# Twelve places for tiles of V, the statistics of the first four steps placed one by one in SP's queue, and a new order of the run-in

## The reference

```python
x = x + attention(layernorm(x)); x = x + fp4_ffn(layernorm(x))
x = x + mixer_and_mlp(x);        x = x + time_mix_ffn(layernorm(x))

q, k, v = (h @ w for w in (w_q, w_k, w_v))          # 2048 x 1024 each, 16 heads of 64
allowed = same segment of 64 | (|i - j| a multiple of 4, 0 < |i - j| <= 256)
out = softmax(q k^T / 8 where allowed) v @ w_o
```

## Time and profile before

| | us |
|---|---|
| median of 3 runs | 515.27 |
| lowest, highest | 514.61, 518.27 |
| the profiled execution | 517.63 |
| its span, first to last instruction | 515.6 |
| TensorE busy, share of the span | 453.7, 88% |
| VectorE busy | 419.0, 81% |
| ScalarE busy | 349.9, 68% |
| GpSimd busy | 312.2, 61% |
| mean granted clock of TensorE | 0.977 of full speed |

### The profile page before, as it was taken

The page is one execution under the profiler, slowest core; times in us unless marked ns, Lnnn a source line. Parts: engine busy times, 40 slices in busy tenths (PEclk is TensorE's granted clock), DMA queues, the critical chain, the costliest instruction groups (busy, mean ns, idle before and its releaser), DMA issues.

```text
span 515.6 us, 17268 instructions
## 1 busy us (share of the span) xinstructions
PE 453.7 (88%) x6418; PEld 352.5 (68%) x6418; DVE 419.0 (81%) x1335; ACT 349.9 (68%) x1021; POOL 312.2 (61%) x497
## 2 busy tenths in 40 slices
PE   0899799999999999999999999989668789768996
PEld 0677577877878778778778788778335456346775
DVE  4865579897899999999999878868899977959135
ACT  3377468867777677677677687754534578786865
POOL 4123447777567577577576865555543789986420
PEclk9999899999999999999999999989879989989999
DMA  6267862346353353453464544540000000000002
GB/s 204 97 188 225 231 193 46 67 91 127 68 108 70 67 107 67 86 101 77 96 134 102 109 106 95 103 87 1 1 0 1 0 1 1 1 0 3 2 0 81
DMA packets 136099, 40.53 MB, mean 79 GB/s; under 512 B 104976, under 2 KB 131024, under 8 KB 136016
## 3 DMA queue, kind: packets, MB, share of 16 engines
q1 hardware_dynamic: 135440, 38.38, 32.2%
q10 hardware_dynamic: 576, 1.05, 0.5%
HBM read 29.44 MB, written 9.96 MB: 76 GB/s over the span
## 4 chain that ended last, share of the span: by engine, by line
PE 42%; DVE 28%; POOL 7%; issue 6%; ACT 6%; DMA 6%; SPq 4%; DVEq 0%; ACTq 0%; POOLq 0%
PE psum L449 6%; PE psum L407 5%; DVE pband L696 4%; PE psum L1153 4%; PE psum L469 3%; DVE pt L757 3%; PE psum L483 3%; PE psum L388 3%; PE psum L495 3%; PE psum L480 2%; DMA w_rows_dram<-st 2%; ACT pband L553 2%; DMA st<-w_rows_dram 2%; DVE area L1555 2%; PE psum L390 2%
## 5 line engine op out<-in xcount | busy, mean ns | idle before, releaser
L929 POOL TENSOR_SCALAR pband<-pband,fac 128x192 f32<-128x192 f32 x256 | 104.6, 429 | 98.7 <-DVE fac L748 98.6
L553 ACT ACTIVATE pband<-pband,st 128x192 f32<-128x192 f32 x256 | 113.2, 448 | 0.3 <-DVE st L696 0.3
L696 DVE CUSTOM_DVE_ANT_0 pband<-psum,band_mask 128x192 f32<-128x192 f32 x256 | 76.0, 353 | 2.6 <-PE psum L407 2.6
L407 PE MATMUL psum<-keys,q_class 64*64 64x192 f32 (+2 forms) x1536 | 66.3, 275 | 0.0
L449 PEld LDWEIGHTS psum<-ident,pband 128*128 128x128 f32 x384 | 45.2, 141 | 23.5 <-issue 18.0
L407 PEld LDWEIGHTS psum<-keys,q_class 64*64 64x64 f32 x1536 | 57.5, 133 | 2.3 <-issue 2.3
L449 PE MATMUL psum<-ident,pband 128*128 128x128 f32 x384 | 53.1, 274 | 3.9 <-DVE pt L757 3.9
L911 POOL COPY keys<-k_rows 128x512 f32<-128x512 f32 x32 | 36.6, 1143 | 24.2 <-issue 14.5
L553 ACT ACTIVATION_READ_ACCUMULATOR pband<-pband,st 128x1 f32 x256 | 49.3, 193 | 0.0
L757 DVE COPY pt<-psum 128x512 f32<-128x512 f32 x64 | 43.8, 684 | 2.0 <-PE psum L449 1.8
L919 POOL COPY q_class<-q_rows 128x512 f32<-128x512 f32 x32 | 36.2, 1131 | 10.3 <-ACT q_rows L593 10.3
(11 more groups left out here) (206 smaller groups left out, 1159.0 us busy)
## 6 DMA issues: line engine op xcount, KB each, us to landing
v_rows_dram<-arena SPq DMA_DIRECT2D x32, 256.0 KB, 3.3
v_both<-v_rows_dram SPq DMA_DIRECT2D x32, 256.0 KB, 3.7
v_seg<-v_rows_dram SPq DMA_DIRECT2D x64, 128.0 KB, 3.6
v_side<-v_rows_dram SPq DMA_DIRECT2D x96, 64.0 KB, 2.6
w_rows_dram<-st SPq DMA_DIRECT2D x64, 8.0 KB, 2.9
st<-w_rows_dram SPq DMA_DIRECT2D x64, 8.0 KB, 2.5
arena<-_attn_hidden_states_dram SPq DMA_DIRECT2D x4, 256.0 KB, 4.4
out_dram<-x SPq DMA_DIRECT2D x4, 256.0 KB, 2.5
```

What stands on the lines that cost most here:

```text
L407: return pe.matmul(bank[2 * r + head][rows, at:at + y.shape[1]], x, y, start=True, stop=True, skip_group_check=True)
L553: act.activation(x, x, ACT.Exp, bias=mine[:, head:head + 1], scale=-1.0, accum_out=mine[:, 2 + head:3 + head]).then_inc(s_exp, 1)
L696: dve.tensor_tensor_reduce(pband[:, G % P_SLOTS, c, head, :], bank[2 * r + head][:, at:at + BAND], band_mask[:, (0, 1, 1, 2)[w], SEG * (1 ...
L929: pool.tensor_scalar(x, x, fac[:, F % 2, 1, c, head:head + 1], 1.0, ALU.mult, ALU.mult).then_inc(s_scaled, 1)
```

## The change

`V_SLOTS` goes from 8 to 12. The four new places are the last 2048 columns of `arena`, behind w_q and w_k; `v_slot(i)` gives the place of a tile. Exchanges 2 and 3 leave SP's loop, which now begins at step 4; `send_statistics` and `fetch_statistics` of the steps 0 to 3 each have a place of their own among the stores and loads. The run-in's queues on all five engines get a new order. No operation is added or left out; each engine issues the same instructions, and `take_values(i)` waits for the store of tile i - 12 in place of i - 8.

```diff
--- before.py
+++ after.py
@@ -65,7 +65,7 @@
 PLAIN = 5 + 1 + 4 + 4 + 3
 W_ROWS = 3 * FT + PLAIN * P
 HALF_HD = HD // 2
-V_SLOTS = 8
+V_SLOTS = 12
 PT_SLOTS = 3
 P_SLOTS = 4
 ROW_SLOTS = 3
@@ -162,7 +162,6 @@
     x_in = pband[:, 2:4, :, :, :].rearrange("p s c h x -> p (s c h x)")[:, 0:NT * D].rearrange("p (n d) -> p n d", d=D)
     xc = pseg[:, 2:4, :, :, :].rearrange("p s a h x -> p s a (h x)")
     wv = pt[:, 0:2, :]
-    v_sb = arena[:, 0:V_SLOTS * 512].rearrange("p (k f) -> p k f", k=V_SLOTS)
     w_qk = arena[:, 4096:4096 + 2 * HD].rearrange("p (k f) -> p k f", k=2)
     wv_hi, wv_lo = w_hi[:, :, HALF_HD:HD], w_lo[:, :, HALF_HD:HD]
     raw = arena[:, 4096:4096 + 3 * FT].rearrange("p (m f) -> p m f", m=3)
@@ -208,6 +207,12 @@
 
         return i % NT, i // NT
 
+    def v_slot(i):
+
+        k = i % V_SLOTS
+        at = HALF_HD * k if k < 8 else 4096 + 2 * HD + HALF_HD * (k - 8)
+        return arena[:, at:at + HALF_HD]
+
     def there(n):
         return 0 <= n < NS_ALL
 
@@ -254,7 +259,7 @@
                 n, half = v_tile(i)
                 sp.wait_ge(s_vev[i % 2], i // 2 + 1)
                 sp.dma_start(v_rows[P * n:P * (n + 1), HALF_HD * half:HALF_HD * (half + 1)],
-                             v_sb[:, i % V_SLOTS, :]).then_inc(s_vst[i % V_SLOTS], 16)
+                             v_slot(i)).then_inc(s_vst[i % V_SLOTS], 16)
 
             def stored(half, w):
                 for i in range(NT * half + TW * w, NT * half + TW * (w + 1)):
@@ -309,21 +314,19 @@
             with nc.allow_non_contiguous_dma(reason="a column of 128 numbers"):
                 for k, v in enumerate(columns):
                     sp.dma_start(constants["cols"][:, k:k + 1], v.rearrange("(p o) -> p o", o=1)).then_inc(s_cols, 16)
-            store_v(0); store_v(1); store_v(2); store_v(3); store_v(4); store_v(5); load_own(0, 0); store_v(6)
-            store_v(7); store_v(8); load_own(0, 1); load_sides(0, 1); store_v(9); store_v(10); store_v(11)
-            store_v(12); store_v(13); load_own(0, 2); load_sides(0, 2); send_statistics(0); store_v(14); store_v(15)
-            store_v(16); store_v(17); store_v(18); store_v(19); fetch_statistics(0); store_v(20); store_v(21)
-            send_statistics(1); store_v(22); load_own(0, 3); load_sides(0, 3); load_wo(); fetch_statistics(1)
-            store_v(23); store_v(24); store_v(25); store_v(26); store_v(27); store_v(28); store_v(29); store_v(30)
-            store_v(31)
+            store_v(0); store_v(1); store_v(2); store_v(3); store_v(4); store_v(5); store_v(6); load_own(0, 0)
+            store_v(7); store_v(8); store_v(9); load_own(0, 1); store_v(10); load_sides(0, 1); send_statistics(0)
+            store_v(11); store_v(12); store_v(13); store_v(14); fetch_statistics(0); store_v(15); store_v(16)
+            store_v(17); load_own(0, 2); send_statistics(1); load_sides(0, 2); load_own(0, 3); load_sides(0, 3)
+            load_wo(); fetch_statistics(1); store_v(18); send_statistics(2); store_v(19); store_v(20); store_v(21)
+            store_v(22); store_v(23); store_v(24); store_v(25); store_v(26); store_v(27); fetch_statistics(2)
+            store_v(28); store_v(29); store_v(30); store_v(31); send_statistics(3); fetch_statistics(3)
             at = 0
-            for F in range(FIRST_STEP - 4, NS_ALL):
+            for F in range(NW, NS_ALL):
                 send_statistics(F)
-                if F >= NW:
-                    load_own(F // NW, F % NW)
+                load_own(F // NW, F % NW)
                 fetch_statistics(F)
-                if F >= NW:
-                    load_sides(F // NW, F % NW)
+                load_sides(F // NW, F % NW)
                 if F == RAW_STEP:
                     sp.wait_ge(s_zero, 1)
                 if F in (RAW_STEP, RAW_STEP + 1):
@@ -496,14 +499,14 @@
 
             pe.wait_ge(s_con, 2)
             pe.wait_ge(s_const, CONST)
-            turn_rows(0); values(0); values(1); turn_rows(1); values(2); project(0, 1); values(3); project(1, 1)
-            values(4); values(5); turn_rows(2); project(0, 0); values(6); values(7); turn_rows(3); values(8)
-            scores(0, 0); values(9); project(2, 1); values(10); project(1, 0); values(11); values(12); scores(0, 1)
-            values(13); project(3, 1); values(14); values(15); scores(1, 0); project(2, 0); values(16); values(17)
-            project(4, 1); values(18); values(19); scores(1, 1); scores(2, 0); values(20); values(21); project(3, 0)
-            values(22); values(23); scores(2, 1); values(24); values(25); project(5, 1); values(26); values(27)
-            project(4, 0); values(28); values(29); scores(3, 0); values(30); values(31); project(5, 0); turn(0, 0)
-            scores(3, 1); turn(0, 1); turn(0, 2)
+            turn_rows(0); values(0); values(1); turn_rows(1); values(2); project(0, 1); values(3); values(4)
+            project(1, 1); turn_rows(2); values(5); values(6); project(0, 0); values(7); values(8); project(2, 1)
+            scores(0, 0); project(1, 0); turn_rows(3); values(9); values(10); scores(0, 1); values(11); scores(1, 0)
+            project(3, 1); values(12); values(13); scores(1, 1); values(14); project(2, 0); values(15); values(16)
+            values(17); project(4, 1); values(18); values(19); scores(2, 0); values(20); values(21); project(3, 0)
+            values(22); values(23); project(5, 1); scores(2, 1); scores(3, 0); values(24); values(25); project(4, 0)
+            values(26); values(27); scores(3, 1); values(28); values(29); project(5, 0); values(30); values(31)
+            turn(0, 0); turn(0, 1); turn(0, 2)
 
 
 
@@ -621,7 +624,7 @@
             def take_values(i):
                 act.wait_ge(s_vmm[i % 2], i // 2 + 1)
                 wait(act, s_vst[i % V_SLOTS], 16 * (i // V_SLOTS))
-                act.copy(v_sb[:, i % V_SLOTS, :], turn_bank[i % 2][:, :]).then_inc(s_vev[i % 2], 1)
+                act.copy(v_slot(i), turn_bank[i % 2][:, :]).then_inc(s_vev[i % 2], 1)
 
             for kind in (1, 0):
                 act.dma_start(w_qk[:, kind, 0:HALF_HD], (w_q, w_k)[kind][:, 0:HALF_HD]).then_inc(s_wqk[0], 16)
@@ -630,14 +633,14 @@
             act.wait_ge(s_const, CONST)
             act.activation(eps[:, 1:2], eps[:, 0:1], ACT.Sqrt)
             split_qk(0, 1); split_qk(0, 0); split_v(0); deviations(0); split_v(1); take_hi(0); deviations(1)
-            take_values(0); take_hi(1); take_values(2); take_keys(0); deviations(2); deviations(3); take_keys(1)
-            take_values(4); take_hi(2); take_queries(0); take_values(6); take_hi(3); take_values(8); take_keys(2)
-            take_values(10); band_exps(0, 0); take_queries(1); take_values(12); band_exps(0, 1); take_keys(3)
-            take_values(14); seg_exps(0); take_queries(2); take_values(16); band_exps(1, 0); take_values(18)
-            take_keys(4); seg_exps(1); take_values(20); band_exps(1, 1); take_queries(3); take_values(22)
-            exp_difference(0); take_values(24); take_keys(5); take_values(26); band_exps(2, 0); take_values(28)
-            seg_exps(2); take_queries(4); take_values(30); band_exps(2, 1); exp_difference(1); take_queries(5)
-            odd_turned(0, 1); band_exps(3, 0); take_keys(6); odd_turned(0, 3); seg_exps(3); band_exps(3, 1)
+            take_values(0); take_hi(1); deviations(2); take_values(2); take_keys(0); take_values(4); take_keys(1)
+            take_hi(2); deviations(3); take_values(6); take_queries(0); take_values(8); take_keys(2); take_queries(1)
+            take_hi(3); band_exps(0, 0); take_values(10); seg_exps(0); band_exps(0, 1); take_values(12); take_keys(3)
+            band_exps(1, 0); take_values(14); seg_exps(1); take_queries(2); take_values(16); band_exps(1, 1)
+            take_keys(4); take_values(18); exp_difference(0); take_values(20); take_queries(3); take_values(22)
+            band_exps(2, 0); take_keys(5); seg_exps(2); take_values(24); band_exps(2, 1); take_values(26)
+            take_queries(4); take_values(28); take_queries(5); exp_difference(1); take_values(30); odd_turned(0, 1)
+            take_keys(6); seg_exps(3); odd_turned(0, 3); band_exps(3, 0); band_exps(3, 1)
             for t in range(FIRST_STEP, DRAIN):
                 exp_difference(t - 4)
                 take_out(t - 6)
@@ -762,7 +765,7 @@
                 cols = acc[:, U % NW * WT:(U % NW + 1) * WT]
                 dve.wait_ge(s_mix, U + 1)
                 if U < NW:
-                    dve.wait_ge(s_vst[U], 16 * V_TILES // V_SLOTS)
+                    dve.wait_ge(s_vst[U], 16 * len(range(U, V_TILES, V_SLOTS)))
                     dve.tensor_copy(cols, shared_bank[:, :]).then_inc(s_acc, 1)
                 else:
                     dve.wait_ge(s_acc, U - NW + 1)
@@ -810,7 +813,7 @@
             def take_values(i):
                 dve.wait_ge(s_vmm[i % 2], i // 2 + 1)
                 wait(dve, s_vst[i % V_SLOTS], 16 * (i // V_SLOTS))
-                dve.tensor_copy(v_sb[:, i % V_SLOTS, :], turn_bank[i % 2][:, :]).then_inc(s_vev[i % 2], 1)
```

(23 more changed lines are left out.)

## The result

| | before | changed |
|---|---|---|
| median of 20 runs, us | 517.16 | 514.06 |
| lowest, highest | 514.61, 520.74 | 510.26, 516.88 |
| the profiled execution, us | 517.63 | 513.94 |
| its span | 515.6 | 512.2 |
| start of round 6 and of round 7 | 68.60, 78.40 | 66.79, 75.49 |

The ratio is 0.9934, with a 95% interval of 0.9911 to 0.9957: 3.4 us gained by the ratio (3.1 between the medians), where 6.0 were forecast. With more runs the kernel before stands at 517.16, so the forecast of 509.3 from 515.27 is a ratio of 0.988, and even the upper end of its range, 512.6, is one of 0.995. The measured ratio lies within that, but the measured time of 514.06 us lies above the range, since that started from a median of three runs that was 1.9 us low.

A forecast was written before the change was run, and what follows sets the result against it. TensorE bounds the kernel, with holes at the run-in's end and in round 6. Gone 1.16 + 2.66 + 1.9 + 0.7 + 1.6 = 8.0, new 0.9 + 1.1 = 2.0, net 6.0: 515.27 to 509.3 us, range 507.3 to 512.6.

The forecast's parts named there:

- the walk: Run-in and first rounds: SP's new order followed with durations from the profile; loop begins at 64.0, round 7 at 72.2 to 72.4.
- both old holes and their slow clock: TensorE's waits for uncopied V tiles until 52.25 and 57.33: 1.16 and 2.66 us, plus 1.9 of slow clock, all to go.
- The pauses around 38 to 41 us: TensorE waits for copies of tiles 12, 13 and 14 behind ScalarE's table load and first exponentials; cost 0.9, bounds 0 and 2.
- the step of round 6: Exchange 2, sent at 57 and back at 67.5, no longer holds turn(1, 2); the 1.59 us hole goes.
- Stores 18 and 19: End of run-in: store 19 lands at 62.0, TensorE waits 1.1 us for tile 31 before turn(0, 1); bounds 0.3 and 2.8.
- Exchange 1: Run-in: sent at 46.7, fetched at 55.5, back at 59.1, ahead of take_values(30) due at 60.0; no cost.
- the clock, a term put at nothing: New pauses at 38 to 41 or 61.7 could bring back the half clock, 1.9 us less gain; not counted.
- store 19 or exchange 1 is late: Rival, end of run-in: slower SP issue, TensorE waits over 3 us, round 6 starts at 1.2 GHz; gain 3.0, 512.3; chance 0.17.
- Exchange 3: Loop: sent at 70.5, back at 77.5; VectorE waits 1.3 us, hidden by TensorE's own round, without that cover 1.3.
- Given back in the loop: Rival, round 7 or 8: exchange 3, VectorE's lag or loads leave only the run-in's gain of 4.5, 510.8; chance 0.10.

The follow-up runs named there:

- w_o_later: The changed kernel with the w_o load moved behind store 21 instead of ahead of the fetch of exchange 1; ratio to the kernel before 0.992.
- exchange_2_early_old_order: The kernel before with one edit: exchange 2 sent ahead of store 27 and fetched ahead of store 31; ratio to the kernel before 0.9977.
- both_and_exchange_2_early: As both_early, with exchange 2 sent after load_own(0, 3), fetched ahead of w_o and stores 20 to 27, exchange 3 sent ahead of store 28; ratio 0.9866.
- best_again: The kernel both_and_exchange_2_early run once more, beside the changed kernel on one chip; ratio to the kernel before 0.9827, median 509.9 us.
- both_early: The changed kernel with stores 18 and 19 and the fetch of exchange 1 ahead of the loads of window 3; ratio to the kernel before 0.9924.

## Why the prediction was wrong

**Right: what bounds the run-in, and the walk up to 60 us.** Twelve places and exchange 0 sent at 38.7 (forecast 38.5) and back by 45.5 (46.0) removed both old holes and their slow clock. The pauses around 38 to 41 us that I priced at 0.9 came to 0.2 (0.18 before 41.90). TensorE was through its last tile at 60.5 and would have been ready for `turn(0, 1)` at about 60.9, 0.8 us ahead of the walk, and the step of round 6 was right as well: exchange 2 no longer holds it.

**Wrong: the size of the step "Stores 18 and 19".** It had the right wait in the right place, priced at 1.1 us with bounds of 0.3 and 2.8. It measured 4.06 us (3.42 and 0.64). What ends the two holes is tile 31: it was to be in its place at 62.7 and was there at 65.05 (64.36 and 0.69 for the copy). Of these 2.3 us, 2.2 are SP, which reached store 19 at 60.18 instead of 58.0, and 0.1 is the landing (4.1 us instead of 4.0). The other 0.8 is that TensorE was ready sooner, which lengthens the hole and not the time. Store 18 landed in 4.6 us, at 63.2, so that most of the standing fell before `turn(0, 0)`, where the walk had none.

**Why SP was late.** The send of exchange 1 was 0.9 us late (47.64 against 46.7): 0.2 at the start of the send of exchange 0, and 0.7 in its first transfer, which took 1.22 us to issue. It did not wait for data, since the exponentials of step 1 were done at 44.1 and those of step 0 at 37.3. Another 0.7 is the side loads of window 2, which took 3.31 us to issue instead of 2.6, 1.4 of it for one load; the rest is in small differences. The walk took the shorter of two rows that it had shown, 2.60 and 3.51. In the ten profiles with the new order these four loads took 2.5 to 4.5 us, and over 3.3 in eight of them, while the four of window 3 took 2.5 to 2.6 in all.

**The step "Exchange 1" was right only by cover.** It said "No cost". Exchange 1 was back at 61.3 instead of 59.1, but store 18 landed later still, so it added nothing here. It is a wait of its own, though: with the stores moved away and this one left, the hole stayed at 4.05; with this one moved and the stores left, at 5.90; only both edits close it.

**Wrong: the clock, a term put at nothing.** The forecast itself had no slow clock in it, on the row of a pause of 1.59 us. The hole grew to 4 us and it came back: from 62 to 68 us it is 0.77. By the rows before, a hole of 2.66 us had already brought it, so the 2.8 us that I named as the bound should have carried 1.9 us of slow clock with it, 4.7 in all. What the slow clock cost here is less: 0.7 us more for the eight transpositions, and 0.6 for the projection behind them (0.43 us a matmul in the chain of work instead of 0.23). So the rule of the Trainium skill, "TensorE: Matmul & The Clock Gate", section "What's actually happening", that the throttled state is the default and activity releases it, had its part in the loss. The trace agrees with it after 3.4 and 4.6 us of hole. How short a pause is enough, the length alone does not say: one of 1.44 us left the full clock (`w_o_later`), two of 1.04 and 1.23 close together did not (`exchange_2_early_old_order`).

**Two readings that do not change the sum.** TensorE's row of the page has a 9 around 77 us and not an 8; the hole of round 6 shows only in the timeline. And the earlier trace rows do not say when the exponentials of step 2 were done: in the trace of the kernel before the last of them ends at 67.2, so exchange 2 could have gone some 2.7 us before 69.97, but not ahead of the nine stores from 62.83.

**The sum again, by what was measured:** round 6 began 1.8 us earlier instead of 4.6, round 7 2.9 us earlier instead of 6.1, and the span is 3.4 us shorter. The missing 3.2 us at round 7 are 2.3 for tile 31, 0.4 from tile 31 to round 6 (1.7 us with the slow transpositions, where the walk had 1.3) and 0.6 for the slow projection of round 6, less 0.1 to 0.2 in small differences. The rival "store 19 or exchange 1 is late" had the mechanism and 3.0 us of gain: store 19 at 64 to 64.5 (64.27 measured), over 3 us of standing, round 6 begun at 1.2 GHz. It is what happened, and I gave it 0.17. Exchange 3 was sent at 74.30, later than the 70.5 of the walk, and was hidden: VectorE came to it at 81.07 and did not wait at all. "Given back in the loop" did not happen; the experiment with exchanges 2 and 3 in the loop shows what it would have looked like.

**The level.** The range was set around the median of three runs. Twenty runs of the kernel before lie between 514.61 and 520.74 us, so three of them fix a level only to about 2 us, and I had left no room for that.

## What to carry to other kernels

Where a chain of waits ends a stage, removing the first one uncovers the next: here places, exchange 0, stores 18 and 19, exchange 1, exchange 2 and exchange 3 lay one behind the other, and most single edits measured nothing or less than nothing. List all waits that would come due at the same time and move them together. In a queue that only issues for 15 us, a small urgent transfer (8 KB of statistics, a store that frees a place) has to stand ahead of loads that nobody needs for 10 us more. A hole that may grow as long as one that brought the slow clock in a trace at hand (here 2.66 us) must be priced with the slow clock behind it. And before start times of two profiles are compared, find a point ahead of the change in both: here up to 1.9 us of such differences were there before the change could act.

## What the runs showed of the hardware

SP needed 0.32 to 0.71 us to issue most of these transfers, and single ones took 1.2 to 1.6 us. The size hardly mattered: 0.60 us for the 512 KB of w_o at 56.82, 0.58 for 8 KB at 57.47. Eight or nine stores of 256 KB in a row took 4.6 to 7.0 us to issue, 0.6 to 0.8 each, which at 256 KB is some 330 to 430 GB/s. The profiles show 317 and 339 GB/s moved from 62 to 68 us, at a DMA share of 0.98 and 1.07. Such stores landed in 3.8 to 5.3 us in the changed kernel, against 2.0 for the first six of the kernel before. Store 18 behind the load of w_o landed in 3.3 us in one profile and in 4.6 to 5.6 in four, and issuing the four side loads of window 2, shortly ahead of it, had taken 2.49 us in the one and 3.3 to 4.2 in the four.

Holes from 2.66 to 7.94 us on TensorE were followed by 1.2 GHz in the matmuls behind them. Single pauses of 1.44, 1.45, 1.59 and 2.06 us were not, but the two of 1.04 and 1.23 us with 0.9 us of work between them were. After the hole of 5.07 us, round 7 took 11.31 us instead of 9.26 though TensorE was busy all the time.

The time behind the attention differs between executions, of one kernel too. From round 31 to the end it took 210.5 to 214.7 us in the thirteen profiles, though no edit touches that part, and 212.5 and 214.1 in the two profiles of one kernel (`both_and_exchange_2_early`, `best_again`). The kernel `both_early` was 4.5 us ahead of the kernel before at round 31 by its profile and 3.3 at the end. The cause stays open. Together with the unequal starts it is why a difference of up to 4 us between two single spans shows nothing here, and why the ratios rest on all runs.
